# Second attention: the softmax denominators come out of the value products, are shuffled over partitions, and the output projection is issued later

## What is computed

```python
q = (x @ q_w).reshape(B, S, 16, 8).transpose(0, 2, 1, 3) * sigmoid(unity_scale)
k, v = ...
scores = einsum('bhqd,bhkd->bhqk', q, k) / sqrt(8)
scores = where((j % 4 == 0) | (|i - j| <= 8), scores, -inf)
attn = softmax(scores, axis=-1)
out = einsum('bhqk,bhkd->bqhd', attn, v).reshape(B, S, 128) @ o_w + o_b
```

## Time and profile before

| what | us |
|---|---|
| runs of the kernel, median of 3 | 1727.6 (1726.49 to 1728.92) |
| span of the profiled execution, first to last instruction | 1723.8 |
| median of the runs less that span | 3.8 |
| TensorE busy with matmuls | 1629.9 |
| VectorE busy | 986.2 |
| ScalarE busy | 987.3 |
| GpSimd busy | 828.9 |

### The profile page before, as it was taken

One profiled execution on the slowest core, in us unless ns is written; L12 is line 12 of the kernel. 1 busy time (PEld: TensorE's weight loads), 2 busy tenths in 40 slices (PEclk: granted clock), 3 DMA queues, 4 the chain that ended last, 5 costly groups with the idle time before them and its releaser, 6 DMA issues.

```text
span 1723.8 us, 49824 instructions
## 1 busy us (share of the span) xinstructions
PE 1629.9 (95%) x19349; PEld 1175.9 (68%) x19353; DVE 986.2 (57%) x2085; ACT 987.3 (57%) x2039; POOL 828.9 (48%) x906
## 2 busy tenths in 40 slices
PE   7999999999999999999998899898988999999995
PEld 5545454555547999998777566565656999997664
DVE  6788898777772222223999676454544222224887
ACT  5667666667664444444555465555555444445773
POOL 7343687877773454552122102555553555553323
PEclk9999999999999999999999899999999999999999
DMA  9900003000016777873342100111112223322434
GB/s 312 416 18 2 16 28 98 28 28 28 30 37 178 234 231 229 234 230 100 110 134 80 52 3 14 36 36 35 36 34 55 83 86 95 86 74 75 125 101 118
DMA packets 172423, 170.05 MB, mean 99 GB/s; under 512 B 20800, under 2 KB 139584, under 8 KB 169248
## 3 DMA queue, kind: packets, MB, share of 16 engines
q1 hardware_dynamic: 152768, 128.84, 24.9%
q0 software_dynamic: 16832, 34.64, 5.9%
q10 hardware_dynamic: 2592, 3.38, 0.7%
HBM read 97.16 MB, written 69.63 MB: 97 GB/s over the span
## 4 chain that ended last, share of the span: by engine, by line
PE 76%; DVE 7%; issue 5%; POOL 4%; another core or an unknown queue 3%; ACT 3%; DMA 1%; SPq 0%; POOLq 0%; DVEq 0%; ACTq 0%
PE ps L1848 14%; PE ps L1839 13%; PE ps L1641 10%; PE ps L1665 4%; PE ps L1605 4%; PE ps L1887 3%; PE ps L1875 3%; PE ps L1732 3%; PE ps L1798 3%; PE ps L1769 3%; PE ps L1606 2%; PE ps L1802 2%; PE ps L1779 2%; DVE s_RS L1318 2%
## 5 line engine op out<-in xcount | busy, mean ns | idle before, releaser
L605 POOL DMA_INDIRECT xd<-s_XN,s_slots x256 | 251.1, 981 | 143.8 <-issue 78.1
L793 ACT ACTIVATE s_S<-ps 128x512 f32<-128x512 f32 x384 | 209.9, 595 | 146.5 <-PE ps L1641 133.6
L1495 DVE TENSOR_TENSOR s_PP<-ps,s_S 128x1024 f32<-128x1024 f32 x192 | 234.4, 1221 | 85.4 <-PE ps L1641 52.8
L1641 PE MATMUL ps<-s_QM,s_KK 32*128 32x512 f32 x1536 | 241.6, 638 | 3.7 <-ACT s_S L793 3.6
L1318 DVE TENSOR_REDUCE s_RS<-ps 128x8 f32<-128x1024 f32 x128 | 150.7, 1218 | 160.6 <-PE ps L1736 85.3
L859 ACT ACTIVATE s_PX<-ps,s_scl 128x1024 f32<-128x1024 f32 x128 | 135.7, 1111 | 186.0 <-PE ps L1779 186.0
L622 POOL DMA_INDIRECT yd<-s_Y,s_to x142 | 136.1, 959 | 137.5 <-DVE s_to L1431 109.6
L874 ACT ACTIVATE s_HH<-ps,s_LG 128x256 f32<-128x256 f32 x284 | 123.6, 474 | 136.8 <-PE ps L1839 135.5
L638 POOL TENSOR_SCALAR_AFFINE_SELECT s_S<-s_S 128x1024 f32<-128x1024 f32 x128 | 140.7, 1099 | 120.8 <-ACT s_S L793 115.3
L874 ACT ACTIVATE s_XN<-ps,s_b1s 128x256 f32<-128x256 f32 x256 | 113.1, 474 | 126.3 <-PE ps L1839 120.2
L622 POOL DMA_INDIRECT yd<-s_XN,s_to x128 | 122.7, 958 | 129.8 <-DVE s_to L1431 102.6
(11 more groups left out here) (224 smaller groups left out, 3009.5 us busy)
## 6 DMA issues: line engine op xcount, KB each, us to landing
s_W<-in_up_w SPq DMA_DIRECT2D x71, 256.0 KB
s_W<-in_down_w SPq DMA_DIRECT2D x71, 256.0 KB
s_X<-xd SPq DMA_DIRECT2D x135, 132.0 KB
xd<-s_zero SPq DMA_DIRECT2D x16, 1056.0 KB, 18.1
s_YG<-yd SPq DMA_DIRECT2D x32, 256.0 KB, 3.7
s_XN<-yd SPq DMA_DIRECT2D x32, 256.0 KB, 4.0
yd<-s_zero SPq DMA_DIRECT2D x7, 1056.0 KB, 27.9
s_DBt<-in_down_b SPq DMA_DIRECT2D x71, 64.0 KB
```

Source lines behind the costliest of these rows:

```text
L605: e.indirect_dma_start(out=xd, out_offset=bass.IndirectOffsetOnAxis(ap=m.slots[:, k, i:i + 1], axis=0), in_=m.XNp[:, i, 0:C + 1], in_offse ...
L793: e.mul(m.S1[u % 3][:, t * 512:(t + 1) * 512], m.PA[:, t * 512:(t + 1) * 512], 1.0 / 64.0).then_inc(s.ev1, 1)
L1495: e.tensor_tensor(m.PP[u % 4][:], m.PB[u % 2], m.S1[u % 3][:], ALU.mult).then_inc(s.prod, 1)
L1641: return e.matmul(out, m.KK[k][32 * r:32 * r + 32, kind, kc * P:(kc + 1) * P], m.QM[k][32 * r:32 * r + 32, kind, :, qc * P:(qc + 1) * P], ...
```

## The change

The ones move into the stationary operand of the values. Besides a head's 8 value columns its block of 32 now has 8 columns of ones, 16 columns away (`values_ones`, GpSimd, once for each of the two buffers). Heads 0 and 1 of a group (`hp` = 0) go to columns 0 to 255 of bank 6, heads 2 and 3 to columns 256 to 511. So in either half of the bank some partitions hold numerators and the others denominators, and a denominator lies 16 partitions away from its numerator.

ScalarE takes the bank times a mask of the upper 16 of each 32 partitions into `SEC` (`second_halves`). VectorE puts denominators together (`DEN`) and numerators (`NUM`) by two operations, each reading half of the bank and half of `SEC`, shuffles `DEN` by 16 partitions within each 32, takes the reciprocal and multiplies. On TensorE `output_second` stands behind `maxima_pe(t+1, 1)` and no longer ahead of it.

```diff
+def values_ones(e, m, s, k):
+
+    e.memset(m.VN[k][:], 0.0).then_inc(s.zv, 1)
+    e.wait_ge(s.zv, 3 * k + 1)
+    for at in (16, 64):
+        e.memset(view(m.VN[k][:], at, [[128, 16], [40, 2], [1, 8]]), 1.0).then_inc(s.zv, 1)
...
+def second_halves(e, m, s, b):
+
+    e.wait_ge(s.wv, 2 * b + 2)
+    if b >= 1:
+        e.wait_ge(s.yn, b)
+    e.mul(m.SEC[:], m.PS[6][:, 0:512], m.second_half).then_inc(s.sec, 1)
...
+        if 1 <= t < NB and t - 1 != MOE_AFTER:
+            second_halves(e, m, s, t - 1)
         if t < NB:
             exponents(e, m, s, t, 0)
...
+        if t == NB:
+            second_halves(e, m, s, NB - 1)
         if t == MOE_AFTER:
+            second_halves(e, m, s, t)
             expert_act(e, m, s, m.x1, 1, ACT.Relu, lambda i, j: m.b1s[:, i // 8, j:j + 1])
...
-def divide_second(e, m, s, b):
-    e.wait_ge(s.wv, 2 * b + 2)
-    e.reciprocal(m.RC[:], m.PS[6][:, 256:512]).then_inc(s.rec, 1)
-    e.wait_ge(s.rec, b + 1)
+def divide_second(e, m, s, o, b):
+
+    first, second = m.PS[6][:, 0:256], m.PS[6][:, 256:512]
+    e.wait_ge(s.sec, b + 1)
+    den = o.mark(e.scalar_tensor_tensor(m.DEN[:], second, m.first_half, m.SEC[:, 0:256], ALU.mult, ALU.add))
+    o.mark(e.scalar_tensor_tensor(m.NUM[:], first, m.first_half, m.SEC[:, 256:512], ALU.mult, ALU.add))
+    o.wait(den)
+    o.mark(e.stream_shuffle(m.RC[:], m.DEN[:], [i ^ 16 for i in range(32)]))
+    o.wait()
+    o.mark(e.reciprocal(m.RC[:], m.RC[:]))
+    o.wait()
     if b >= 1:
         e.wait_ge(s.o1, b)
-    e.tensor_tensor(m.YC[:], m.PS[6][:, 0:256], m.RC[:], ALU.mult).then_inc(s.yn, 1)
+    e.tensor_tensor(m.YC[:], m.NUM[:], m.RC[:], ALU.mult).then_inc(s.yn, 1)
...
         for qb in range(4):
             for c in range(4):
-                e.matmul(P4[32 * c:32 * c + 32, qb * 64:qb * 64 + 64], m.VN[b % 2][:, qb, 4 * c + hh, :],
-                         PX[:, c, x * 256 + qb * 64:x * 256 + qb * 64 + 64],
-                         start=(hh == 0 and qb == 0), stop=(hh == 3), skip_group_check=True)
-        for c in range(4):
-            i = e.matmul(P4[32 * c:32 * c + 32, 256:512], m.ON[:, hh, :], PX[:, c, x * 256:x * 256 + 256],
-                         start=False, stop=(hh == 3), skip_group_check=True)
+                i = e.matmul(P4[32 * c:32 * c + 32, hp * 256 + qb * 64:hp * 256 + qb * 64 + 64], m.VN[b % 2][:, qb, 4 * c + hh, :],
+                             PX[:, c, x * 256 + qb * 64:x * 256 + qb * 64 + 64],
+                             start=(hh == 0 and qb == 0), stop=(x == 1), skip_group_check=True)
     i.then_inc(s.wv, 1)
...
+        if t + 1 < NB:
+            maxima_pe(e, m, s, t + 1, 1)
         if t >= 1 and t - 1 != MOE_AFTER:
             output_second(e, m, s, t - 1)
-        if t + 1 < NB:
-            maxima_pe(e, m, s, t + 1, 1)
```

More of the change, by code:

```diff
@@ L419, in semaphores @@
         "scl_a", "scl", "max", "maxv", "neg", "mturn", "mvt"))
-    s.sc, s.ex, s.wv, s.rec, s.yn, s.o1, s.given = (sem(n) for n in ("sc", "ex", "wv", "rec", "yn", "o1", "given"))
+    s.sc, s.ex, s.wv, s.sec, s.yn, s.o1, s.given = (sem(n) for n in ("sc", "ex", "wv", "sec", "yn", "o1", "given"))
     s.zg = [sem(f"l_zg{k}") for k in range(NF)]
@@ L718, in gpsimd_program @@
         if g == NG - 7:
-            for x in (m.VN[0], m.ON):
-                e.memset(x[:], 0.0).then_inc(s.zv, 1)
-            e.wait_ge(s.zv, 2)
-            e.memset(view(m.ON[:], 0, [[40, 4], [1, 8]]), 1.0).then_inc(s.zv, 1)
+            values_ones(e, m, s, 0)
         if g == NG - 5:
-            e.memset(m.VN[1][:], 0.0).then_inc(s.zv, 1)
+            values_ones(e, m, s, 1)
         if g == NG - 3:
@@ L2093, in _constants @@
         sm[:, 154 + j] = (np.arange(P) // 8) % 4 == j
+    sm[:, 158] = (np.arange(P) // 16) % 2 == 0
+    sm[:, 159] = (np.arange(P) // 16) % 2 == 1
     c["c_small"] = sm
```

21 lines of the change are left out of this document (12 added, 9 removed).

## The result

The changed kernel took **1715.73 us** (median of 5 runs, 1712.35 to 1722.05) against 1727.6 (median of 5, 1723.28 to 1728.92) on the same chip: 11.9 us less by the medians. The ratio over all runs is 0.9945, 95% interval 0.9922 to 0.9968, by which the gain is 9.5 us. Forecast were 1707, 20.8 less: the kernel is faster, by about half of what was forecast.

The account below looks back on a forecast made before the run. TensorE, busy 95% of the span, was taken as the bound, with VectorE arriving together with it at the output. Savings 1 + 4 + 14 + 1.5 + 1.5 less 1.2 gave 20.8 us, from 1727.6 to 1707; range 1699 to 1720.

Parts of the forecast that it names:

- my own case: The whole kernel: the summed forecast of 1707 us, reaching from 1701 to 1713, chance 0.70.
- rival 2: VectorE's chain is late by 0.4 us per iteration, 30 times: about 1719 us, spread 1712 to 1728; chance 0.09.
- iterations 7 to 20: Second attention beside GpSimd's scatters: TensorE's pauses stay, 1.0 us saved in each iteration, 14 us in all.
- Iterations 21 and 22: Around the experts: two shorter `weigh` count, the third is given back to VectorE's longer chain; 1.5 us saved.
- Iterations 23 to 30: Behind the experts: `weigh` waits for L1352 behind VectorE's combining, periods 13.6 three times and 14.2 five times; 1.5 us saved.
- The end: The last division stands alone on the path and its chain is longer: 1.2 us lost.
- Clean iterations: Undisturbed iterations of the second attention's batch loop: period from 14.17 to 13.04 us, 1.13 saved each.
- The move: Output projection behind the second maxima, no longer in the exponentials' shadow: costs 0.59 us per clean iteration.
- rival 3: TensorE is bound by records, so the ones were cheap: 5.4 us saved in 32 iterations, 1723 us; chance 0.04.
- VectorE's chain: Division on VectorE, from sums through shuffle and reciprocal to product: 3.41 us in place of 2.20, just in time for the output.
- rival 4: The shuffle costs 1.75 us like the reciprocal, the chain is 1.33 longer: slower, 1740 us; chance 0.05.
- Rival 1: TensorE's pauses in `weigh` beside the scatters shrink with the records: 6.5 us more gained, 1700 us; chance 0.10.

Follow-up runs that it names:

- move_only: The kernel before with only the output projection moved behind the second maxima, products of ones kept: 1679.32 us, ratio 1.0025 to the kernel before.
- shuffle_twice: The changed kernel with the shuffle in the division's chain done twice: 1715.98 us, beside 1708.72 for the changed kernel on the same chip.
- light_after: The changed kernel with the second expert's share left out of the combining of pairs: 1646.4 us, against 1668.96 for the kernel before with the same edit.
- after_again: The changed kernel as it is, on another chip: 1708.72 us against 1721.63 for the kernel before, ratio 0.9927.
- before_again: The kernel before, unchanged, run again for its profile on a second chip: 1721.0 us, ratio 0.9998 to its own runs there.
- after_same: The changed kernel as it is, on a second chip: 1708.84 us against 1721.56 for the kernel before, ratio 0.9928.
- early_end: The changed kernel with second halves scaled before the last tanh and the last division before the last gating and offset: 1706.42 us, against 1708.84 without this edit.

## Why the prediction was wrong, step by step

The time, 1715.73, lies inside the stated range of 1699 to 1720, but this confirms nothing: it is outside my own case (1701 to 1713), the range reaches there for the sake of rival 2, which did not happen, and of the gain of 20.8 about half came. What failed are terms of the sum, those of iterations 7 to 20, 21 and 22, 23 to 30 and of the end, and the clock, which was no term.

- **Clean iterations: right.** 13.07 for 13.04. That it is so near is luck in part, since terms were off and cancel. The move costs 0.18 alone (move_only), not 0.59. But the first scores start 0.35 later than forecast: the shortened `weigh` now ends before the signal of the first reductions is there, which I had checked for the second half of the iteration alone. And the next maxima come 1.46 behind the exponentials, not 1.37. 0.18 + 0.35 + 0.09 is 0.62 beside the 0.59 of the sum. The ones were worth 0.43 per group of 8, so rival 3 is out; a `weigh` of 80 records went from 1.89 to 1.03 with 64, as the columns say. The rule of the Trainium skill (TensorE: Matmul & The Clock Gate, "Wait — 56ns, not 53.3ns?") would have brought 0.4 per `weigh` and is not borne out by these rows.
- **VectorE's chain: right.** The shuffle took 0.44 (forecast 0.42), so rival 4 is out; the estimate of 0.30 worked out from the Trainium skill (VectorE: DVE Perf Modes, "The perf-mode tier table") is too low. The pass of ScalarE took 0.69, not 0.59, hidden in clean iterations. "Just in time" was literal: shuffle_twice passes 0.47 on in full as 0.48.
- **Iterations 7 to 20, 14 us: wrong for this chip.** "1.0 each, the pauses stay" held nearly for twelve ordinary iterations (0.8 each on the first chip, 0.9 on the second) and for a chip without pauses (14.7 in all). It failed in iterations 8 and 15, forecast -2, measured +3.5 on the first chip (+2.4 and +1.1) and +0.9 on the second. In 15 the waits end in a stretch at half clock, without which it gains 1.3 to 1.6. Iteration 8 holds a wait of 2.8 for late exponentials that no fewer records shorten, so that it gains nothing at full clock either, and on the first chip, with a wait of 3.7 and 6.8 us at half clock behind it, it takes 2.2 more. What makes these signals late stays open.
- **The clock was no term of the sum.** I took it as 1.00 from the earlier trace rows. The changed kernel's runs have 0.0055 less of it on average, an estimated 4 us, rather less. That half clock follows TensorE's waits is seen in the rows, and in one place by filling a wait, where it cost nothing. Its price is seen in iterations 15 (1.1) and 26 (1.2); the 4 us as a whole are argued.
- **Iterations 21 and 22, -1.5: wrong, +0.6 and -0.5.** Iteration 21 gains 0.7 to 0.8; iteration 22, which holds the experts, is 0.3 to 1.3 longer. On the first chip TensorE waits 1.46 for the product there and 3.4 at half clock follow; whether this sets its length wasn't tried.
- **Iterations 23 to 30, -1.5: wrong, +0.8 to +1.2.** Two things. The wait for L1352 was right: it is done at 9.40 and 10.00, forecast 9.33 and 9.94. But I let `weigh` start at once behind it and the scores 1.03 later; it starts 0.15 behind, and the scores 1.24 behind `weigh`, since the reductions, too, stand behind the keeping. So the periods are 13.9 and 14.5 to 14.8, not 13.6 and 14.2, and iterations 24, 25 and 27 to 30 change by +0.2 and -0.4 in all. That VectorE's work is the bound there is shown by light_after, whose periods are 13.0 to 13.8. The second thing is iteration 26, +1.9 and +2.0 in these profiles: a longer wait and then half clock; iteration 23 gains 0.9 to 1.0. In after_again, on another chip with pauses, iteration 26 is 15.02 at full clock, below the 15.2 and 15.4 of the kernel before, and b 23 to b 31 is 117.2, against before_again's 118.4: without that one piece the stretch is near its forecast.
- **The end, +1.2: wrong, +3.0 to +3.9.** The chain itself grew by 1.26, as forecast (before_again's 1.79 from the reciprocal's start to the product's, after_same's 3.05 from L1363's). The rest is ahead of it: from b 31 to the last combining it is 27.9 and 29.7, and of this 1.8 the late first reductions are 1.6. The clock doesn't set it: 29.7 with 10.2 us of half clock in after_same, 29.6 with 3.4 in early_end.
- **Rival 2** (the chain late by 0.4 per iteration, 1719) came nearest in time, which is chance: clean iterations are not late. Rival 1 falls too, as the pauses did not shrink (12.2 and 11.6).
